# Attention: in each slot TensorE computes the coming unit's scores before it transposes the last unit's probabilities

## What is computed

```python
q = _rope((xn @ q_w + q_b).reshape(b, s, H, HD).transpose(0, 2, 1, 3), theta)
k = _rope((xn @ k_w + k_b).reshape(b, s, H, HD).transpose(0, 2, 1, 3), theta)
v = (xn @ v_w + v_b).reshape(b, s, H, HD).transpose(0, 2, 1, 3)
scores = jnp.einsum('bhqd,bhkd->bhqk', q, k) * scale
scores = jnp.where(causal, scores, -jnp.inf)
attn = jax.nn.softmax(scores, axis=-1)
ctx = jnp.einsum('bhqk,bhkd->bhqd', attn, v)
attn_out = ctx.transpose(0, 2, 1, 3).reshape(b, s, H * HD) @ o_w + o_b + xn
```

## Time and profile before

| | |
|---|---|
| median of 3 runs | 2507.6 us (2507.32 to 2508.99) |
| profiled execution: its own time | 2507.55 us |
| profiled execution: span in the trace | 2505.6 us |
| mean granted TensorE clock | 0.916 of full speed |
| busy, share of the span | PE 82%, PEld 54%, DVE 67%, ACT 57%, POOL 37% |

### The profile page before, as it was taken

One profiled execution on the slowest core, in us unless ns is written; L12 is line 12 of the kernel. 1 busy time (PEld: TensorE's weight loads), 2 busy tenths in 40 slices (PEclk: granted clock), 3 DMA queues, 4 the chain that ended last, 5 costly groups with the idle time before them and its releaser, 6 DMA issues.

```text
span 2505.6 us, 41253 instructions
## 1 busy us (share of the span) xinstructions
PE 2063.1 (82%) x10326; PEld 1363.4 (54%) x10326; DVE 1666.8 (67%) x2947; ACT 1440.3 (57%) x2785; POOL 920.0 (37%) x797
## 2 busy tenths in 40 slices
PE   3749999879675999987966699996996669999698
PEld 1236666547324666655732466664662256666466
DVE  3957676669485666647948666674794766666488
ACT  2517676647542766655744366674674346766366
POOL 1544343223164434313315444341332453434222
PEclk9879999979796999997979799999897979999899
DMA  2000000001000000001100000000110000000011
GB/s 60 0 26 5 9 8 0 1 28 40 10 0 26 10 5 8 0 1 34 34 10 0 26 10 5 8 0 9 30 30 10 13 14 8 9 4 0 11 34 32
DMA packets 36210, 35.48 MB, mean 14 GB/s; under 512 B 3992, under 2 KB 30976, under 8 KB 36096
## 3 DMA queue, kind: packets, MB, share of 16 engines
q1 hardware_dynamic: 36096, 34.14, 4.7%
HBM read 32.03 MB, written 2.10 MB: 14 GB/s over the span
## 4 chain that ended last, share of the span: by engine, by line
PE 59%; DVE 20%; issue 10%; ACT 5%; POOL 4%; DVEq 1%; ACTq 0%; DMA 0%; POOLq 0%; SPq 0%
PE ps L1341 10%; PE ps L1180 7%; PE ps L1181 7%; PE ps L1182 7%; PE ps L1330 6%; DVE state L930 6%; PE ps L1320 4%; PE ps L1321 4%; PE ps L1356 3%; PE ps L1448 2%; PE ps L1208 2%; DVE q_split L993 2%; PE ps L1172 2%; DVE bx L923 2%; DVE ps L1008 1%
## 5 line engine op out<-in xcount | busy, mean ns | idle before, releaser
L707 ACT ACTIVATE probsT<-ps 128x512 f32<-128x512 f32 (+3 forms) x768 | 349.6, 493 | 382.4 <-PE ps L1330 381.7
L695 ACT ACTIVATE probs<-ps,least 128x640 f32<-128x640 f32 (+7 forms) x512 | 380.6, 743 | 65.4 <-DVE least L1003 59.5
L1330 PE MATMUL ps<-ident,probs 128*128 128x128 f32 x2304 | 349.4, 279 | 10.4 <-ACT probsT L707 10.2
L1320 PE MATMUL ps<-k_high,q_split 128*128 128x512 f32 (+3 forms) x768 | 309.2, 403 | 57.8 <-POOL k_low L550 38.6
L1330 PEld LDWEIGHTS ps<-ident,probs 128*128 128x128 f32 x2304 | 262.9, 141 | 128.2 <-issue 91.6
L538 POOL TENSOR_TENSOR roped<-turned 128x512 f32<-128x512 f32 x128 | 192.6, 1506 | 286.1 <-DVE turned L978 274.2
L1341 PE MATMUL ps<-probsT,vals 128*64 128x512 f32 (+3 forms) x1536 | 290.4, 502 | 5.2 <-ACT probsT L707 5.2
L1003 DVE CUSTOM_DVE_ANT_0 ps<-ps,row_masks 128x128 f32<-128x128 f32 (+3 forms) x256 | 127.6, 499 | 235.2 <-PE ps L1321 232.5
L1010 DVE TENSOR_REDUCE least<-ps 128x1 f32<-128x640 f32 (+3 forms) x256 | 262.3, 1025 | 9.1
L1321 PE MATMUL ps<-k_low,q_split 128*128 128x512 f32 (+3 forms) x768 | 259.0, 349 | 0.0
L755 ACT ACTIVATE hid<-ps,cols 128x512 f32<-128x512 f32 x256 | 176.4, 689 | 105.2 <-PE ps L1182 77.1
(11 more groups left out here) (213 smaller groups left out, 4252.2 us busy)
## 6 DMA issues: line engine op xcount, KB each, us to landing
w<-in_w SPq DMA_DIRECT2D x128, 128.0 KB, 2.0
w_pair<-in_w_pairs SPq DMA_DIRECT2D x36, 256.0 KB, 2.7
xin<-in_x SPq DMA_DIRECT2D x5, 512.0 KB, 3.9
out<-acc SPq DMA_DIRECT2D x4, 512.0 KB, 4.1
pos<-in_c_pos SPq DMA_DIRECT2D x1, 512.0 KB, 5.5
v_w<-in_v_w SPq DMA_DIRECT2D x1, 512.0 KB
o_w<-in_o_w SPq DMA_DIRECT2D x1, 512.0 KB
v_b<-in_v_b SPq DMA_DIRECT2D x1, 512.0 KB
```

Of the source, the lines that this page charges most:

```text
L695: act.activation(probs[:, t % 2, 0:width(t)], banks(2 * (t % 2))[:, 0:width(t)], ACT.Exp, bias=least[:, t:t + 1], scale=-1.0, accum_out=ro ...
L707: act.activation(dst, ps[:, T_BANK + g % 2, 0:k1 - k0], ACT.Copy).then_inc(t_taken, 1)
L1320: pe.matmul(o, q, k_high[par][h][:, k0:k1], start=True, stop=False)
L1330: made = pe.transpose(ps[:, T_BANK + g % 2, at - k0:at - k0 + P], probs[:, t % 2, at:at + P], ident[:, :])
```

## The change

In `step` of TensorE the two calls `scores` and `turn_probs` change places. The head of each slot, and all the other engines' instructions, keep their order. In the last step's slot 3 `global_sums` stands ahead of both now.

```diff
-                        if t > 0:
-                            turn_probs(n, t - 1)
-                        elif not first:
-                            turn_probs(n - 1, UNITS_A - 1)
                         if last and t == SUM_SLOT:
                             global_sums(b + 1, 1)
                         if t + 2 < UNITS_A:
                             scores(n, par, t + 2)
                         elif not last:
                             scores(n + 1, 1 - par, t + 2 - UNITS_A)
+                        if t > 0:
+                            turn_probs(n, t - 1)
+                        elif not first:
+                            turn_probs(n - 1, UNITS_A - 1)
```

## The result

| | before | changed |
|---|---|---|
| median | 2508.3 us (4 runs, 2507.3 to 2512.0) | 2780.6 us (4 runs, 2776.7 to 2783.0) |
| profiled execution: own time, span | 2507.55, 2505.6 | 2776.66, 2774.7 |
| mean granted TensorE clock | 0.916 | 0.914 |

The ratio is 1.108 (95% interval 1.106 to 1.110): 272 us slower. The forecast was 2795.6 us, 288 us slower, with a range of 2738 to 2860.

The account below looks back on a forecast made before the run. TensorE was taken to bound each 40.3 us step; 11.75 us of new waiting less 2.7 old gave 9.0 a step, times 32 steps 288 us, added to 2507.55 for 2795.6 us, range 2738 to 2860.

Parts of the forecast that it names:

- The chain: Between slots: transposes done, ScalarE's copy, exponentials, next scores; up to 2.08 us, with only the slot's head beside it.
- Rival 3: Earlier scores give VectorE and ScalarE a start and TensorE's waits go: faster, 2421 us; chance 2%.
- The sum of a step: Chain less head (the slot's other TensorE work) over 12 slots: 11.75 us new waiting, less 2.7 old, net 9.0.
- the lower bound: Copy sometimes held by ScalarE's earlier work, so chain 0.15 us shorter in 12 slots: 7.2 us a step, 2738 us.
- Clock 1.00 in attention: Expected sign in the profile after: TensorE's granted clock stays at 1.00 throughout attention.
- rival 4: Pauses drop TensorE's clock in attention from 1.00 to 0.50; a quarter of steps at half clock, 3096 us; chance 3%.
- The row of the scan: Scan, 30 us: 67 matmuls at 0.23 us, some 15.4 us of work, granted 1.00 despite pauses; evidence against clock loss.
- First and last steps: First and last step of each sequence also taken at 9.0 us, with an error of a few us a sequence.
- The rest of the trace, state space and experts, is unchanged: Outside attention the change was to alter nothing in the trace.
- rival 1: Only slots 0, 13, 14, 15, with little or no cover, stall: net 3.2 us a step, 2608 us; chance 6%.
- Covered slots: Slots 3, 5, 7 and 11: heads at least as long as the chain, so 0 us of new waiting.

Follow-up runs that it names:

- 5: Changed kernel with one more 128x128 copy on ScalarE ahead of every exponential; 2906.9 us.
- 6: Kernel before the change with one more 128x128 copy on ScalarE ahead of every exponential; 2534.8 us, ratio 1.0111.
- 10: Changed kernel with the second half of the next pair's values moved from slot 10 to slot 15; 2782.4 us.
- 8: Changed kernel with one unread 128x512 product on TensorE ahead of the scores in each of slots 13 and 15; 2763.8 us, 1.101 of the kernel before.
- 3: Changed kernel, except that the last step of each sequence keeps the old order; 2753.6 us.
- 1: Kernel before with scores put ahead of transposes only in slots 3, 5, 7 and 11, which have long heads; 2541.0 us, ratio 1.0125.
- 2: Kernel before with scores put ahead of transposes only in slots 13 and 15, which have no head; 2544.1 us, ratio 1.0134.
- 11: Kernel before with second half of values moved from slot 10 to 15, and slot 14's output projection put behind the transposes; 2443.3 us, ratio 0.973.
- 9: Kernel before with the second half of the next pair's values moved from slot 10 to slot 15; 2465.8 us, ratio 0.984.

## Why the prediction was right

**The chain.** This was right, and shown: the links stand in the timeline, ScalarE's added work costs some 2.8 times as much in the changed order once the time at half clock is made equal (5, 6), and cover moved from one slot to another leaves a step at 48.3 us (10). Rival 3, the gain, had nothing for it.

**The sum of a step.** Measured from start to start in the step at full clock, the pauses were, with the prediction's figure behind each: slot 0 0.55 (0.72), 1 0.36 (0.38), 2 0.38 (0.38), 4 0.51 (0.59), 6 0.72 (0.80), 8 1.17 (1.25), 9 0.65 (0.73), 10 0.89 (1.04), 12 0.56 (0.69), 13 1.91 (1.99), 14 1.02 (1.10), 15 2.10 (2.08). All twelve places were right and no other paused. The sum is 10.8 against 11.75. With the old waits of 2.7 gone, this gives 8.1 us a step, and 48.33 - 40.3 = 8.0 was measured. The term "chain less head" was sized 0.9 us a step too high, but not for the reason given with the lower bound, that the copy is sometimes held by ScalarE's earlier work. Ahead of the copy in all six rows that were read ScalarE was idle; the earlier trace rows show two, and the others are

```profile
311.58 0.49 ACT L707 ACTIVATE probsT<-ps 128x384 f32<-128x384 f32 x1 [1.43 <-PE ps L1330]
316.02 0.60 ACT L707 ACTIVATE probsT<-ps 128x512 f32<-128x512 f32 x1 [0.88 <-PE ps L1330]
323.32 0.77 ACT L707 ACTIVATE probsT<-ps 128x512 f32<-128x512 f32 x2 [0.65 <-PE ps L1330]
330.23 0.87 ACT L707 ACTIVATE probsT<-ps 128x512 f32<-128x512 f32 x2 [0.51 <-PE ps L1330]
```

From the copy's start to the end of the accumulator's reading ScalarE takes the same time in both traces, to 0.01 us: 2.07 for slot 15, 1.86 for 13, 1.43 for 0, 1.37 for 8, 1.16 for 6; only slot 10's is shorter, 1.65 instead of 1.78. Most of the rest is on TensorE. The chain was counted from a row of scores behind the transposes, and now a head stands there that starts up to 0.08 us later (0.76 us behind the start of seven transposes, not 0.69), and a projection behind transposes takes 0.78 us, not the 0.70 of the earlier trace rows.

**The clock.** "Clock 1.00 in attention" was wrong. Five of the six steps of the loop, in each of the four sequences, have a stretch at half clock around slots 15 and 0, nearly always of 3.4 us, and are about 49.3 instead of 48.3 us long (8). This is rival 4 in a small form: it was priced with a quarter of all steps at half clock, and came with about 7% of most steps. It nearly made up for the oversized chain in the loop, so the 9.0 us a step that I forecast for the loop were met (295.0 us for six steps against 240.8, 9.0 each; 9.2 in the last two sequences) by luck, two errors of opposite sign. The Trainium skill's page "TensorE: Matmul & The Clock Gate", in its section "A second HAM failure mode: psum-queue depth-cycling", describes such a swing under small pauses; this trace agrees, with 0.53 granted from 323.50 to 326.90 and no pause of TensorE above 2.1 us. The row of the scan on which I relied did not carry over, and the prediction read it wrongly. About half of its 67 matmuls are those of L1250, four in the row below, which stand 0.43 us apart and not 0.23, so that its work is some 22 us of the 30 (33 x 0.43 + 34 x 0.22) and not 15.4:

```profile
92.66 1.88 PE L1250 MATMUL ps<-cs,ident 128*128 128x512 f32 x4
```

The scan was thus about as full as an undisturbed step of the changed kernel, 37.5 of 48.3 us, and its full clock says less against rival 4 than the prediction took from it.

**First and last steps, and the rest.** The closeness of the total is in part luck. Between the two profiled executions the difference is 2774.7 - 2505.6 = 269.1 us. From start to start it divides so, for all four sequences (forecast behind each): the loops 218.6 (216); the first steps, from the first scores to the first weighing of the next step, 42.1 (36); the last steps, from that weighing on, 19.1 (36); all that lies outside, -10.7 (0). "I take both at 9.0 as well, with an error of a few us for a sequence": cut so, the first costs 10.5 and the last 4.8 (6.8 by the whole time of 3). "The rest of the trace, state space and experts, is unchanged" was wrong too: outside the attention TensorE was at half clock for 382.0 us before and 345.5 in the changed kernel, with the same work; whether the 10.7 us come from there was not tried. In the sum for rival 1, 3.2 us a step gives 2610 us, not 2608.

**Covered slots.** In the whole change they pause nowhere, as I had counted. But that they "cost nothing" holds only while the next slot is in the new order too: swapped alone they cost 1.0 us a step (1). Costs of single slots are therefore not terms that can be added up; 1 and 2 together give 2.1 us of the 9.0, for six of the sixteen slots.

## What to carry to other kernels

In an in-order queue, an operation that is ready and feeds another engine goes ahead of one that has to wait for that engine; put behind, it closes a loop in which both take turns idling, although each is busy for well under its time (11 shows no more than that: in slot 14, going ahead of independent work as well gained the loop nothing). To price such a swap, read the length of the other engine's chain from the trace of before, subtract for each place what still lies beside it, and look at the neighbours: cover belongs to a stretch, not to a place. And an idle stretch that remains can be filled by moving a piece of independent work there: the same reading of waits gave 1.6% in the kernel before (9). A total that comes out as forecast is no proof: 10 and 11 look plainer in their medians than in their steps.

## What was not expected of the hardware

TensorE's granted clock fell to its lower level (1.2 of 2.4 GHz) in stretches of 3.4 us though the engine never paused for more than 2.1 us; ahead of the fall in the step from 278.55 stood the three pauses of slots 13 to 15 (1.7, 0.9 and 1.8 us as recorded) with scores, transposes and one output projection between them. One idle-time product of 128x512 in two of the pauses removed it in the loop and made the kernel 17 us faster (8). What such a stretch costs is not fixed: about 1.0 us a step in the changed kernel, 1.6 where only slots 13 and 15 are swapped (43.0 against 41.4 us, in 2) and 1.6 with the values late (50.0 against 48.3 to 48.4 us, in 10).
